# Two products of transposed query and key weights moved ahead of the first queries, into another PSUM bank, and ScalarE's copies reordered

## The reference

```
# token layer
xd    = difference of x along time (0 at t = 0)
emb   = xd @ W_ve.T + b_ve
h     = (ewma(emb) + reversed ewma(emb)) / 2 @ W_lin.T + b_lin
# attention layer, on n = layernorm(h), 4 heads of 32
q, k  = l2norm(n @ Wq), l2norm(n @ Wk);  v = n @ (basis @ v_coeffs.T)
score = (q . k) * decay_h ** max(t_k - t_q - 1, 0) * (t_k > t_q)
h     = h + (score @ v) @ (basis @ o_coeffs.T).T * out_scale
# ffn layer, on n = layernorm(h), lower triangular W1, W2
h     = h + tril(W2) . gelu(tril(W1) . n + b1) + b2
```

## Time and profile before

| what | us |
|---|---|
| median of 3 runs | 79.86 |
| lowest and highest run | 79.47, 82.85 |
| the profiled execution's own time | 79.86 |
| its span, first to last instruction | 78.1 |
| TensorE matmul busy | 69.2 |
| VectorE (DVE) busy | 54.0 |
| ScalarE (ACT) busy | 42.7 |
| GpSimd (POOL) busy | 37.0 |
| mean granted clock of TensorE, share of 2.4 GHz | 0.97 |

### The profile page before, as it was taken

How to read it: one execution, slowest core, us unless ns; L and a number is a source line. 1 busy time by engine, 2 the same in 40 slices (tenths; PEclk the granted TensorE clock), 3 DMA queues, 4 the chain that set the end, 5 groups by cost and what they waited for, 6 DMA issues and landing times.

```text
span 78.1 us, 2783 instructions
## 1 busy us (share of the span) xinstructions
PE 69.2 (89%) x1087; PEld 53.4 (68%) x1087; DVE 54.0 (69%) x175; ACT 42.7 (55%) x97; POOL 37.0 (47%) x50
## 2 busy tenths in 40 slices
PE   4999869995998999969999999999999979959930
PEld 4998658764357667857579867988599956834920
DVE  4888993956058694199955899299963798892340
ACT  1638485379755407897653666565483443665400
POOL 5104988429439646476039240926065000686600
PEclk9999995599999999999999999999999999999996
DMA  0970012121434500000000400022000400004053
GB/s 7 251 252 0 0 33 57 34 50 36 106 78 101 108 18 0 0 13 0 0 0 8 131 0 0 8 59 77 8 0 0 140 4 0 0 0 131 0 158 104
DMA packets 4786, 3.85 MB, mean 49 GB/s; under 512 B 3131, under 2 KB 4149, under 8 KB 4774
## 3 DMA queue, kind: packets, MB, share of 16 engines
q1 hardware_dynamic: 4434, 3.44, 16.3%
q10 hardware_dynamic: 340, 0.24, 1.1%
HBM read 1.00 MB, written 1.54 MB: 32 GB/s over the span
## 4 chain that ended last, share of the span: by engine, by line
PE 66%; DVE 10%; issue 8%; POOL 7%; ACT 5%; DVEq 0%; POOLq 0%
PE s_ps L1120 7%; PE kra_ps L1061 7%; PE s_ps L1033 6%; PE s_ps L1137 6%; PE s_ps L853 5%; PE kra_ps L1087 4%; PE kra_ps L1048 4%; PE s_ps L935 4%; PE kra_ps L991 4%; PE kra_ps L1108 3%; DVE h L766 3%; DVE prob L702 3%; POOL quad L331 2%; POOL h_b L368 2%; PE s_ps L978 2%
## 5 line engine op out<-in xcount | busy, mean ns | idle before, releaser
L702 DVE TENSOR_TENSOR prob<-s_ps,dmask 125x500 f32<-125x500 f32 x24 | 14.8, 671 | 2.5 <-PE s_ps L1033 2.4
L346 POOL TENSOR_TENSOR q_dec<-qT,powers 128x500 f32<-128x500 f32 x5 | 5.8, 1164 | 11.4 <-ACT qT L449 11.4
L368 POOL TENSOR_TENSOR h_b<-h,w_ffn 125x512 f32<-125x512 f32 (+1 forms) x7 | 7.8, 1124 | 5.7 <-DVE h L766 3.5
L479 ACT ACTIVATE xn<-h,rstd 125x128 f32<-125x128 f32 x20 | 6.4, 390 | 4.9 <-POOL rstd L358 4.9
L331 POOL TENSOR_TENSOR quad<-gram_z,z 128x250 f32<-128x250 f32 (+1 forms) x6 | 5.8, 984 | 5.5 <-ACT gram_z L518 3.3
L1061 PE MATMUL kra_ps<-prob,v_sc 125*32 125x125 f32 x192 | 6.8, 272 | 0.9 <-DVE prob L702 0.5
L766 DVE SCALAR_TENSOR_TENSOR h<-kra_ps,rec,h_tok 125x128 f32<-125x128 f32 x24 | 6.8, 343 | 1.0 <-PE kra_ps L1087 1.0
L1033 PE MATMUL s_ps<-qT,kT 32*125 32x125 f32 x192 | 7.3, 290 | 0.1
L752 DVE TENSOR_TENSOR y<-s_ps,h_b 125x512 f32<-125x512 f32 (+1 forms) x6 | 3.9, 647 | 4.8 <-PE s_ps L1137 4.8
L1061 PEld LDWEIGHTS kra_ps<-prob,v_sc 125*32 125x32 f32 x192 | 5.1, 109 | 2.9 <-issue 2.3
L1033 PEld LDWEIGHTS s_ps<-qT,kT 32*125 32x125 f32 x192 | 6.2, 191 | 1.2 <-issue 1.0
(11 more groups left out here) (178 smaller groups left out, 145.1 us busy)
## 6 DMA issues: line engine op xcount, KB each, us to landing
out_dram<-y SPq DMA_DIRECT2D x5, 224.0 KB
z_stk<-z_hi SPq DMA_DIRECT2D x8, 62.5 KB, 2.3
z_stk<-z_hi SPq DMA_DIRECT2D x8, 31.2 KB, 2.0
z_stk<-z_lo SPq DMA_DIRECT2D x4, 62.5 KB, 2.1
out_dram<-y SPq DMA_DIRECT2D x2, 112.0 KB
w_base<-in_w_base_dram SPq DMA_DIRECT2D x1, 192.0 KB, 3.4
w_ffn<-in_w_ffn_dram SPq DMA_DIRECT2D x1, 192.0 KB, 3.4
xt<-in_x_dram SPq DMA_DIRECT2D x1, 188.0 KB, 3.1
```

Of the source, the lines that this page charges most:

```text
L368: pool.tensor_tensor(h2_b[n][:, b0:b1, :], h2[n][:, b0:b1, :], b2_row.unsqueeze(1).broadcast_to([C, b1 - b0, D]), ALU.add)\
L702: dve.tensor_tensor(prob[i % 2][:, h, :, :], sc_ps[h][0:C, 0:W4].rearrange("p (b t) -> p b t", b=B), dmask[:, h, :].unsqueeze(1).broadcast ...
```

## The change

On TensorE, the two products (before at L1144 and L1145) move ahead of `early_qk(0)`, in place of the unread product of L873. They are written to bank k1 in place of bank r. They wait for projc_ok alone; the wait for the bias copy moves to `early_qk(1)`, which overwrites bank r. On ScalarE, the copies of the v and o weights now stand ahead of `high_words(1)`, and the copy of the two products reads bank k1. Nothing is computed differently.

```diff
--- before.py
+++ after.py
@@ -419,12 +419,12 @@
             act.activation(proj_T[:, 0, :], k1_ps[:, 0:STK], ACT.Copy).then_inc(projc_ok, 1)
             act.wait_ge(qkbias_ps, 1)
             act.activation(qk_bias[:, :], r_ps[:, 2 * D:2 * D + 2], ACT.Copy, scale=ONE).then_inc(qkbias_ok, 1)
-            high_words(1)
             act.wait_ge(mix_ps, 1)
             act.activation(v_w[:, :], a_ps[:, 0:D], ACT.Copy).then_inc(vw_ok, 1)
             act.activation(o_T[:, :], a_ps[:, D:2 * D], ACT.Copy, scale=osc).then_inc(oT_ok, 1)
+            high_words(1)
             act.wait_ge(qkT_ps, 1)
-            act.activation(proj_T[:, 1:3, :].rearrange("p a b -> p (a b)"), r_ps[:, 0:2 * STK], ACT.Copy)\
+            act.activation(proj_T[:, 1:3, :].rearrange("p a b -> p (a b)"), k1_ps[:, 0:2 * STK], ACT.Copy)\
                 .then_inc(qkT_ok, 1)
 
             def early_queries(j):
@@ -870,7 +870,9 @@
                 ins = pe.matmul(r_ps[:, 2 * D + n:2 * D + n + 1], wqk_c[:, n * D:(n + 1) * D],
                                 proj[:, B * CH:B * CH + 1], start=True, stop=True)
             ins.then_inc(qkbias_ps, 1)
-            unread(1)
+            pe.wait_ge(projc_ok, 1)
+            pe.matmul(k1_ps[:, 0:STK], wqk[:, 0:D], proj_T[:, 0, :], start=True, stop=True)
+            pe.matmul(k1_ps[:, STK:2 * STK], wqk[:, D:2 * D], proj_T[:, 0, :], start=True, stop=True).then_inc(qkT_ps, 1)
 
 
             TERMS = ((w_hi, z_hi), (w_hi, z_lo), (w_lo, z_hi))
@@ -883,6 +885,7 @@
                 if j == 1:
                     pe.wait_ge(qkT_ok, 1)
                     pe.wait_ge(oT_ok, 1)
+                    pe.wait_ge(qkbias_ok, 1)
                 for n, (col, landed) in enumerate(((Q0, q_s), (K0, k_s))):
                     for term, (weights, words) in enumerate(TERMS):
                         for b in range(B):
@@ -1139,10 +1142,6 @@
                 ins.then_inc(f2_s, 1)
 
             early_qk(0, s_ps)
-            pe.wait_ge(projc_ok, 1)
-            pe.wait_ge(qkbias_ok, 1)
-            pe.matmul(r_ps[:, 0:STK], wqk[:, 0:D], proj_T[:, 0, :], start=True, stop=True)
-            pe.matmul(r_ps[:, STK:2 * STK], wqk[:, D:2 * D], proj_T[:, 0, :], start=True, stop=True).then_inc(qkT_ps, 1)
             early_qk(1, kra_ps)
             scores(0)
             forms()
```

## The result

The changed kernel took 82.31 us median (81.92 to 82.56, 4 runs); the kernel before, beside it, 81.29 (79.47 to 82.85, 4 runs). Both kernels turn out to have two groups of times, one near 79 and one near 82, and the comparison sets the changed kernel's four runs, all of the upper group, against the two of before in the lower one, hence the ratio 1.033 (1.024 to 1.041). My forecast was 79.1, with a range up to 80.3, so the measured time is outside it.

A forecast was written before the change was run, and what follows sets the result against it. TensorE's order was taken as the bound (66% of the chain), with a low clock near 12 to 15.5 us. 79.86 less 0.65 gave 79.2, a moving low stretch 78.8 to 79.05; 79.1 was taken, range 77.6 to 80.3.

The forecast's parts named there:

- (a): TensorE, two products replacing the unread one: early_qk(0) starts 0 to 0.15 us later, 0.05 taken.
- (c): ScalarE's copy of the two products runs beside early_qk(0); first queries' copy starts near 9.3, not 10.10: gain 0.8.
- (e): First scores start at about 10.65 instead of 11.48; grams at 11.95 instead of 13.03, 1.08 us ahead.
- (b): ScalarE: v and o weight copies ahead of high_words(1), which waits for z until 8.73: cost 0, cover 0.3 us.
- (d): early_qk(1), second queries: held latest by low words L646, starts at about 9.5 instead of 10.45; added bias wait costs 0.
- (f): Low clock held fixed from 12.08 to 15.48 us; forms end at 15.8 to 16.0, leaving 0.65 of 1.2 won.
- The rival without a low clock: Low clock over scores, grams and forms doesn't come: 2.05 us won, 77.8; chance 0.25.
- the absorption: DMA or GpSimd, with its own time, takes over and absorbs the gain: 0 to 0.3 won, 79.7; chance 0.13.
- The slower rival: Clock falls earlier and a second low stretch follows from early_qk(1) on, costing 1.05 to 1.3 us: 80.4; chance 0.10.
- The highest run of 82.85: Sign cited for the slower rival: 3 us over the median, so the kernel has expensive states.

The follow-up runs named there:

- after_again: The changed kernel run once more with nothing else altered; 79.75 us median of six runs, profiled execution 78.74.
- after_early: The changed kernel with GpSimd's memset of z_stk's rows moved from behind the masks to ahead of its first wait; 78.98 us.
- before_early_b: Second measurement of the kernel before with GpSimd's memset of z_stk's rows moved ahead of its first wait; 79.01 us median of 10 runs.
- after: The changed kernel as first measured, beside the kernel before; 82.31 us median of four runs, profiled execution 82.56.
- before_forced: The kernel before with VectorE made to wait ahead of L655 for GpSimd's masks, so L655 comes behind the memset's start; 81.68 us median.
- after_forced: The changed kernel with VectorE made to wait ahead of the small addition for GpSimd's masks, so it comes behind the memset's start; 82.16 us.
- after_third: The changed kernel unaltered, measured a third time; 12 runs, eight from 77.77 to 78.94 us and four from 81.17 to 82.12; trace 81.50.
- look_4: Kernel before with GpSimd's memset moved early and an unread 0.89 us VectorE memset ahead of the low weights, fourth extra traced execution; 82.44 us.
- before_early: The kernel before with GpSimd's memset of z_stk's rows moved ahead of its first wait; 79.62 us, 12 runs.

## Why the prediction was wrong, step by step

(a), (c) and (e), the order of work: right where no collision came in. In the lower trace, after_again, the two products cost TensorE nothing (first queries at 8.20), the copy ran beside the first queries, the added wait for the bias cost nothing, and second queries, scores and grams came 0.95, 0.90 and 1.15 earlier. In (a) I named the bound 0 to 0.15, which is a little small: in after_early and before_early_b, where w_hi and the first low words stand at the same times (7.37 and 8.13), first queries start at 8.77 and 8.56, so the products cost 0.2 there.

(b) and (d) are the step that failed, in what they left out. In (b) I gave high_words(1) a cover of 0.3 us and looked only at ScalarE's side. The path to the second queries goes from there to VectorE's L646, and in (d) I made it the latest of the four waits, "The last is the latest now: start at about 9.5", without asking what else VectorE does between z and L646 and beside whom. Measured was 11.88, 2.4 us later, since L655 took 2.07 us and L609 had taken 1.23. The addition L655 stood 0.29 ahead of a 2.6 us memset in the trace of before. I had one execution in which VectorE won the race, and took its 0.26 for the instruction's price; it is 0.16 to 2.6 us.

(f), the low clock: wrong in its choice. I held the stretch from 12.08 to 15.48 as fixed in time and as part of the kernel, from one trace. In the eight traces that have such a stretch it begins anywhere from 10.79 to 13.60, and it lasts 3.4 us in four of them and 6.8 in the other four. In the profiled execution it ran from 11.98 to 18.80, so the forms ended at 19.26 and not at 15.8 to 16.0: 2.4 us of that is the wait ahead of second queries, and about 0.9 the longer low clock. Together they account for the 3.2 us between the forecast and the result. Of the thirteen traces below 80.1 us, the first of before among them, ten have a clock of 0.997 or 1.00; and in four of the five upper ones it is low for twice as long. My factor for a low clock, 1.5 to 2, doesn't follow from the ratios that I named (1.10 to 0.71 is 1.55, 1.55 to 1.15 is 1.35), but it fits what came: 1.78 against 1.15 for the scores, 1.10 against 0.60 for L904. The rival without a low clock, 77.8 with 2.05 won, had the order right and its size a little high: the trace shows 78.74, and the changed kernel's runs with a clock of 1.00 lie from 77.77 to 78.94. In the trace 1.1 us was absorbed, some 0.9 of it in the wait for the first z_stk copies. I had looked at the second batch only, and had ruled out the absorption by its 4.4 us. Not only chunks from the third on read z_stk, as the description of the kernel says: the keys and values of the first two chunks (L991) read the first batch.

The slower rival had a place and a price by the clock alone: 80.4 at a chance of 0.10, for a second stretch from the second queries on. That stretch is there in the trace of after. But the row-tiled products standing together aren't enough for it: in after_again they stand the same way, with a clock of 0.997. What differs is VectorE's wait.

The highest run of 82.85 was the sign that I read too lightly: three microseconds above the median in one of three runs is a group of the kernel's times, here almost half of all runs (35 of 73), and the median of three hid it. These runs don't show that the change made it or took it away (10 of 22). Between the lower groups it wins 0.9 to 1.2% (ratios 0.991 and 0.988). That is a little flattering, since the lower group of the kernel before has some runs with a short low clock and that of the changed kernel none. Between runs with a clock of 0.99 or more it is 0.6 us in the mean (78.41 of 11 runs, 78.97 of 29), beside 0.65 forecast with the low clock and 2.05 without. That the four runs of the first comparison all fell in the upper group has a chance of about 3% if the 10 upper runs of 22 fell anywhere; a condition of that session isn't excluded. Luck works the other way too: the later medians, 79.75 and 78.77, lie within the range that I gave, though the mechanism of (d) and (f) would have been no better understood.

What stays open: what starts the long low clock in the upper runs of the kernel of before with the early memset. One such trace was caught, and it had the delay. How fast TensorE's first products run seems to have a part in it, as the last section shows.

## What to carry to other kernels

Read the spread of the runs before the median: two groups say that somewhere two engines race, and the trace of one execution shows only one outcome. Look in it for small VectorE instructions that start just ahead of a long GpSimd instruction, and give the GpSimd instruction a place where no VectorE instruction has to wait for it (here GpSimd's idle from 2.4 to 6.8 us). A wait of two microseconds on TensorE may be paid a second time by the clock: with the forced collision the clock was low in twelve of twelve runs, with the early memset in 12 of 28 of both kernels. And an advance wins in the end only what the next fixed time leaves: look for the first use of every batch of copies, not of the last one only.

## What was not expected of the hardware

- An addition on 125x4 fp32 numbers on VectorE took 0.16 to 0.26 us alone, and 1.82, 2.07, 2.58 and 2.59 (before_forced, after, after_forced, after_third) behind the start of a GpSimd memset of 2x3000 numbers; each time it ended within 0.05 us of the memset's end.
- The granted clock fell in the executions in which TensorE had waited about 2 us (2.16 in the trace of after, 2.11 in look_4) and stayed at 1.2 GHz for 6.8 us, though TensorE was busy nearly all of that time. In after_third, with a wait of 2.57, it was low for 3.4 us (mean clock 0.970 against 0.954 and 0.952). It also fell, for 3.4 us, behind a longest wait of only 0.62 in the trace of before, while in before_early, with one of 0.63, it stayed at 1.00.
- In after_early a z_stk copy of 31 KB, the last of twelve issued one behind the other, took 3.49 us to land, while the medians for such copies in the same trace are 2.0 (high words) and 2.4 (low words).
- TensorE's product L860, the same in every kernel, took 0.68 to 1.20 us at the start of the span, though the granted clock reads 1.00 there. In the five traces where it took 0.68 to 0.70, GpSimd's subtraction (L306, L308 or L309), which waits behind it by way of ScalarE, started at 6.31 to 6.68, and in four of them it came ahead of the first z (L623, L624) and made it wait. In the other thirteen the subtraction started at 6.81 to 7.25 and this z never waited. The falls of the clock come in the same order: at 10.79 to 11.53 in those four, at 11.98 to 12.13 where L860 took 0.76 to 0.84, at 13.60 in the one trace with 1.20 that has a fall.
